# Plain f32 products for attention's projection and merge in a fused alignment, attention and expert kernel

## The reference

```
h = grad of the soft Needleman-Wunsch value of theta (32 x 128 x 128)
h = h + attention(layernorm(h))
h = h + experts(layernorm(h))        # 8 experts, top 2, silu gated
```

```
Q = einsum('bthd,hd->bht', xh, Wq);  K = einsum('bthd,hd->bht', xh, Wk)
P = softmax(-(Q[:, :, :, None] - K[:, :, None, :]) ** 2 / 4)
O = einsum('bhts,bhse->bhte', P, einsum('bthd,hde->bhte', xh, Wv))
out = O.reshape(B, T, E) @ Wm + x
```

## Time and profile before

| | us |
|---|---|
| median of 3 runs | 842.27 (841.99 to 842.51) |
| the profiled execution, its own time | 846.1 |
| its span | 844.0 |
| TensorE products busy | 484.8 (57%) |
| TensorE weight loads busy | 422.3 (50%) |
| VectorE busy | 593.4 (70%) |
| ScalarE busy | 406.8 (48%) |
| GpSimd busy | 230.7 (27%) |

### The profile page before, as it was taken

The page is one execution under the profiler, slowest core; times in us unless marked ns, Lnnn a source line. Parts: engine busy times, 40 slices in busy tenths (PEclk is TensorE's granted clock), DMA queues, the critical chain, the costliest instruction groups (busy, mean ns, idle before and its releaser), DMA issues.

```text
span 844.0 us, 13480 instructions
## 1 busy us (share of the span) xinstructions
PE 484.8 (57%) x2622; PEld 422.3 (50%) x2623; DVE 593.4 (70%) x2029; ACT 406.8 (48%) x1180; POOL 230.7 (27%) x417
## 2 busy tenths in 40 slices
PE   1200000000004689899899998620899999999960
PEld 0200000000003578798788987610688888888850
DVE  3698989889747866978988674652466666666645
ACT  1344444444302867666666574100566656666630
POOL 1054545455300000000403312455133333333330
PEclk9999999999999999999999999999999999999985
DMA  4499230403254122222102000012111111111109
GB/s 98 90 177 165 45 72 10 82 1 81 41 137 125 51 75 63 63 75 62 52 26 67 26 7 20 26 38 64 35 45 42 44 43 44 41 43 43 44 16 287
DMA packets 113385, 54.18 MB, mean 64 GB/s; under 512 B 56652, under 2 KB 109132, under 8 KB 113251
## 3 DMA queue, kind: packets, MB, share of 16 engines
q1 hardware_dynamic: 106366, 44.60, 22.7%
q0 software_dynamic: 4352, 8.47, 3.0%
q10 hardware_dynamic: 2621, 0.62, 0.5%
HBM read 29.93 MB, written 24.26 MB: 64 GB/s over the span
## 4 chain that ended last, share of the span: by engine, by line
PE 36%; DVE 31%; issue 20%; DMA 5%; SPq 4%; ACT 3%; ACTq 0%; DVEq 0%; POOLq 0%
DVE D L1178 5%; PE ps L541 5%; DVE D L1153 5%; PE ps L543 5%; PE ps L542 5%; PE ps L747 4%; PE ps L627 4%; PE ps L727 4%; PE ps L632 3%; ACT D L819 2%; DVE D L1144 2%; PE ps L746 2%; PE ps L743 2%; DVE rc L1322 2%; DVE ps L1133 1%
## 5 line engine op out<-in xcount | busy, mean ns | idle before, releaser
L1038 POOL DMA_INDIRECT xd_dram<-pay,slot x64 | 64.8, 1013 | 281.3 <-DVE pay L1402 263.9
L632 PEld LDWEIGHTS ps<-va,pt 128*128 128x128 f32 x512 | 137.5, 351 | 0.0
L627 PE MATMUL ps<-eye_sb,sq 128*128 128x128 f32 x256 | 114.8, 454 | 13.9 <-DVE on L1339 10.3
L1064 POOL DMA_INDIRECT y_dram<-on,dest x72 | 70.7, 982 | 164.1 <-DVE on L1482 127.5
L632 PE MATMUL ps<-va,pt 128*128 128x17 f32 x512 | 114.7, 307 | 0.0
L577 PE MATMUL ps<-zdiag,ones_f 32*128 32x32 f32 x2 | 0.6, 406 | 193.0 <-DVE zdiag L1221 193.0
L627 PEld LDWEIGHTS ps<-eye_sb,sq 128*128 128x128 f32 x256 | 87.5, 343 | 34.4 <-issue 25.8
L577 PEld LDWEIGHTS ps<-zdiag,ones_f 32*128 32x128 f32 x2 | 0.5, 304 | 193.1 <-DVE zdiag L1221 193.1
L1022 POOL TENSOR_TENSOR D<-D 128x128 f32<-128x128 f32 x130 | 56.3, 433 | 129.3 <-DVE D L1171 65.0
L1453 DVE TENSOR_TENSOR sq<-sq,ps 128x512 f32<-128x512 f32 x72 | 49.5, 688 | 56.2 <-PE ps L543 41.1
L819 ACT ACTIVATE D<-D 64x2 f32<-64x2 f32 (+1 forms) x154 | 31.4, 204 | 106.9 <-DVE D L1153 86.9
(11 more groups left out here) (226 smaller groups left out, 1474.1 us busy)
## 6 DMA issues: line engine op xcount, KB each, us to landing
stage<-xd_dram SPq DMA_DIRECT2D x72, 65.0 KB, 1.8
D<-th_dram SPq DMA_DIRECT2D x16, 208.0 KB, 4.8
g_dram<-D SPq DMA_DIRECT2D x14, 208.0 KB, 4.6
x_dram<-D SPq DMA_DIRECT2D x14, 208.0 KB, 4.7
h0q<-g_dram SPq DMA_DIRECT2D x8, 256.0 KB, 3.0
gb<-g_dram SPq DMA_DIRECT2D x8, 256.0 KB, 3.5
xf<-x_dram SPq DMA_DIRECT2D x8, 256.0 KB, 3.2
xb<-x_dram SPq DMA_DIRECT2D x8, 256.0 KB, 3.5
```

Of the source, the lines that this page charges most:

```text
L627: last = nc.tensor.transpose(ps[:, 5 + h // 4, T * (h % 4):T * (h % 4) + T], sq[n % 3][:, T * h:T * h + T], eye_sb[:])
L632: m = nc.tensor.matmul(ps[:, 7, (HD + 1) * h:(HD + 1) * (h + 1)], pt[turned % 2][:, T * h:T * h + T], va[q % 2][:, k, h, :], start=True, s ...
L1038: pool.indirect_dma_start(xd_dram, bass.IndirectOffsetOnAxis(slot[:, q, j, k:k + 1], 0), pay[q % 2][:, k, j, :], None).then_inc(s_sc[2 * k ...
L1064: pool.indirect_dma_start(y_dram, bass.IndirectOffsetOnAxis(dest[:, c:c + 1], 0), yrow[c], None, bounds_check=2 * NB * T - 1, oob_is_err=F ...
```

## The change

The operands of `project` and `merge` are no longer split. ScalarE's copies write plain f32 (`xnt`, `ont`), the subtractions `tokens_low` and `heads_low` and their semaphores go, and each block of a quad takes one f32 product: in `merge` with the whole 128 x 128 `wm_sb`, in `project` with a `wqk_sb` of 32 columns whose result goes to partitions 32k to 32k+31 of PSUM, one tile of 32 columns of the array per block. The weights are loaded as they are, `wqk_pl` as 128 x 32 in place of 4 x 128 x 128. TensorE waits once for `wm_sb` before its loop. The expert stage gets buffers of its own instead of the shared ones.

```diff
-        wqk_hi = sb("wqk_hi", [E, 4, 128], fr)
-        wqk_lo = sb("wqk_lo", [E, 4, 128], fr)
-        wm_hi = sb("wm_hi", [E, E], fr)
-        wm_lo = sb("wm_lo", [E, E], fr)
+        wqk_sb = sb("wqk_sb", [E, 32])
+        wm_sb = sb("wm_sb", [E, E])
...
-        xcol_hi = [ont_hi[:, T * k:T * k + T] for k in range(2)]
-        xcol_lo = [ont_lo[:, T * k:T * k + T] for k in range(2)]
+        xcol_hi = [sb(f"xcol_hi{k}", [128, T], fr)[:, :] for k in range(2)]
+        xcol_lo = [sb(f"xcol_lo{k}", [128, T], fr)[:, :] for k in range(2)]
...
-        hidt_hi, hidt_lo = xnt_hi, xnt_lo
+        hidt_hi = [sb(f"hidt_hi{k}", [128, 512], fr) for k in range(2)]
+        hidt_lo = [sb(f"hidt_lo{k}", [128, 512], fr) for k in range(2)]
...
                 pe.wait_ge(s_xnt, q + 1)
-                pe.wait_ge(s_xntl, q + 1)
                 need(pe, s_msk, q - 4)
                 for k in range(4):
-                    c = slice(T * k, T * k + T)
-                    m = three(ps[:, 2, 0:T], (wqk_hi[:, k, :], wqk_lo[:, k, :]), (xnt_hi[r][:, c], xnt_lo[r][:, c]),
-                              k == 0, k == 3)
+                    m = nc.tensor.matmul(ps[32 * k:32 * k + 32, 2, 0:T], wqk_sb[:], xnt[r][:, T * k:T * k + T],
+                                         start=True, stop=True)
...
                     c = slice(T * k, T * k + T)
-                    m = three(ps[:, 1, c], (ont_hi[:, c], ont_lo[:, c]), (wm_hi[:], wm_lo[:]))
+                    m = nc.tensor.matmul(ps[:, 1, c], ont[:, c], wm_sb[:], start=True, stop=True)
...
             pe.wait_ge(s_consts, 5)
+            pe.wait_ge(s_wraw, 1)
...
-            nc.scalar.activation(wqk_hi[:], raw_qk[:], ACT.Copy)
             nc.scalar.activation(below_sb[:], raw_below[:], ACT.Copy)
             act.wait_ge(s_small, 3)
-            nc.scalar.activation(wm_hi[:], ps[:, 1, 0:E], ACT.Copy).then_inc(s_wraw, 1)
+            nc.scalar.activation(wm_sb[:], ps[:, 1, 0:E], ACT.Copy).then_inc(s_wraw, 1)
...
-            dve.wait_ge(s_wraw, 1)
-            V_.tensor_tensor(wqk_lo[:], raw_qk[:], wqk_hi[:].bitcast(f32), ALU.subtract)
-            V_.tensor_tensor(wm_lo[:], ps[:, 1, 0:E], wm_hi[:].bitcast(f32), ALU.subtract)
...
-                quad(heads_low, n, -6)
-                quad(tokens_low, n, 7)
```

More of the change, by code:

```diff
@@ L123, in tower @@
         mz = al("mz", [128, 1])
-        raw_qk = al("raw_qk", [E, 4, 128])
         raw_v = al("raw_v", [E, E])
@@ L162, in tower @@
         xn = [sb(f"xn{k}", [T, 4, T]) for k in range(2)]
-        xnt_hi = [sb(f"xnt_hi{k}", [128, 512], fr) for k in range(2)]
-        xnt_lo = [sb(f"xnt_lo{k}", [128, 512], fr) for k in range(2)]
+        xnt = [sb(f"xnt{k}", [128, 512]) for k in range(2)]
         on = [sb(f"on{k}", [T, 4, T]) for k in range(2)]
-        ont_hi = sb("ont_hi", [128, 512], fr)
-        ont_lo = sb("ont_lo", [128, 512], fr)
+        ont = sb("ont", [128, 512])
         x3t = sb("x3t", [128, 512])
@@ L256, in tower @@
         s_thw = [sem(f"s_thw{c}") for c in range(BLKS)]
-        s_xntl = sem("s_xntl")
-        s_ontl = sem("s_ontl")
         s_qkh = sem("s_qkh")
@@ L641, in turn_heads @@
                 pe.wait_ge(s_xnt, min(q + 4, NQ))
-                pe.wait_ge(s_xntl, min(q + 4, NQ))
                 need(pe, s_x3t, q - 1)
@@ L650, in merge @@
                 pe.wait_ge(s_ont, q + 1)
-                pe.wait_ge(s_ontl, q + 1)
                 need(pe, s_h1, q)
@@ L661, in turn_inputs @@
                 pe.wait_ge(s_ont, min(q + 2, NQ))
-                pe.wait_ge(s_ontl, min(q + 2, NQ))
                 need(pe, s_rkc, q)
@@ L680, in ranks @@
                 pe.wait_ge(s_ont, min(q + 3, NQ))
-                pe.wait_ge(s_ontl, min(q + 3, NQ))
                 nc.tensor.matmul(ps[:, 0, 0:32], below_sb[:], msk[:, :, :].rearrange("p b e -> p (b e)"),
@@ L788, in _ @@
                 act.dma_start(dst, src).then_inc(s_in, 16)
-            for dst, src in ((raw_qk[:], wqk_pl.rearrange("g e c -> e g c")), (raw_v[:], wv_bd), (raw_m[:], w_m),
+            for dst, src in ((wqk_sb[:], wqk_pl), (raw_v[:], wv_bd), (raw_m[:], w_m),
                              (wg_sb[:], w_g), (eye_sb[:], eye), (raw_below[:], below), (mask_sb[:], head_mask),
@@ L873, in tokens_high @@
                 need(act, s_qkp, q - 1)
-                nc.scalar.activation(xnt_hi[q % 2][:], ps[:, 0, :], ACT.Copy).then_inc(s_xnt, 1)
+                nc.scalar.activation(xnt[q % 2][:], ps[:, 0, :], ACT.Copy).then_inc(s_xnt, 1)
             def values(q):
@@ L910, in heads_high @@
                 need(act, s_rp, q)
-                nc.scalar.activation(ont_hi[:], ps[:, 0, :], ACT.Copy).then_inc(s_ont, 1)
+                nc.scalar.activation(ont[:], ps[:, 0, :], ACT.Copy).then_inc(s_ont, 1)
             def copy_inputs(q):
@@ L1300, in first_norms @@
                 V_.tensor_tensor(h1[:, 4 * q:4 * q + 4, :], h[:], x1[q % 2][:], ALU.add).then_inc(s_hx, 1)
[L1302 to L1306, removed]
             def queries_keys(q):
@@ L1340, in normalise @@
                                  over(rc[:, 1, :], HD), ALU.mult).then_inc(s_on, 1)
[L1342 to L1345, removed]
             def residual(q):
@@ L1533 @@
     NH, HD = wq.shape
-    wqk_pl = np.zeros((4, 128, 128), wq.dtype)
+    wqk_pl = np.zeros((128, 32), wq.dtype)
     wv_bd = np.zeros((128, 128), wv.dtype)
@@ L1538 @@
         r = slice(HD * h, HD * h + HD)
-        for g in range(4):
-            for part in range(2):
-                wqk_pl[g, r, 32 * g + NH * part + h] = wq[h]
-                wqk_pl[g, r, 32 * g + NH * (2 + part) + h] = wk[h]
+        for part in range(2):
+            wqk_pl[r, NH * part + h] = wq[h]
+            wqk_pl[r, NH * (2 + part) + h] = wk[h]
         wv_bd[r, r] = wv[h].T
```

## The result

The new kernel takes 823.88 us (median of 4 runs, 822.7 to 824.96) against 842.38 (4 runs, 841.99 to 842.51) on the same chip: ratio 0.9781, 95% interval 0.9764 to 0.9798, 18.5 us faster. I had put 832.6, in a range from 828 to 838.5. The direction was right; the gain was nearly twice the 9.7 that I had worked out.

What follows compares the result with a forecast made beforehand. Attention was taken as bound in turns by TensorE (around project) and VectorE (from an odd turn's end through the norms). Gains 4.8+6.0-1.1 = 9.7 us off the median 842.27 gave 832.6 us, range 828 to 838.5.

Steps and rivals of the forecast that it cites:

- VectorE's low parts: Attention: dropping VectorE's two subtractions per quad shortens waits before turns 1, 2, 6, 10, 14, 18; gain 4.8 us.
- 1.1+0.6+1.0: Gains in us from dropping the tokens' subtraction in quads 0, 1 and 2, at the start of attention.
- the four gaps: TensorE's idle gaps before turns 6, 10, 14, 18, expected to close by 0.42, 0.60, 0.52, 0.60 us.
- I take four back to back: Project on TensorE: four narrow products at 0.36 us each, slot 1.74 instead of 2.73; 6.0 us saved over six intervals.
- 0.72 less 0.27: Project: price of a narrow product began from a 0.72 us f32 product, less 0.27 for one moving column versus 128.
- the rival on the column tiles: Project: the four column tiles overlap, slot 0.93 us, total gain 12.6, time 829.7; chance 0.22.
- so 0.72: Merge: one plain f32 product costs 0.72 us, read from the setup; merge 0.3 longer, 1.1 us lost in all.
- The lower bound that I had given, 0.45: Merge: lowest price in us considered for one plain f32 product, from a setup product with one moving column.
- The cap of 1.17: Intervals after turns 14, 18, 22, where VectorE also does `choose`: project's gain limited to 1.17 us each.
- What I said of hiding: Merge's extra 0.3 us hidden after turn 7, 0.17 showing after turns 11, 15, 19; setup savings and last merge hidden.
- The end is paced by the sends: End of attention: last norms wait 5.54 us for GpSimd's sends; what counts is how much earlier turn 31 is done.
- The clock rival: Attention: TensorE's clock rises as plain f32 products stream longer, some 20 us gained, time 822; chance 0.05.

Runs made afterwards that it cites:

- e14: New kernel with the merge as two fp32r terms, the heads' low part left out, five executions beside the unchanged new kernel: 824.6 us, ratio 0.9805.
- e6: New kernel with project as four plain f32 products of all 128 columns, weights zero-padded, no column tiles: 830.3 us, ratio 0.9868.
- e4: New kernel plus five series of eight products in TensorE's idle time of the alignment, to price product kinds: 829.8 us in one execution, ratio 0.980.
- e2: Kernel before with only the merge made plain f32 and the heads' subtraction dropped; project keeps three terms and its subtraction: 842.8 us, ratio 0.9949.
- e10: New kernel plus 40 plain f32 products in TensorE's idle time ahead of the experts, on a slower chip: 830.2 us, ratio 0.9808.
- e11: New kernel with VectorE's subtraction of the heads and its waits put back, result unread, the tokens' one left out: 833.7 us, ratio 0.9839.
- e5: New kernel with the merge as two fp32r terms, the heads' low part left out, first run: 826.3 us, ratio 0.9824.

## Why the prediction was wrong

The ledger of the starts of turns, trace of before against e14 (its merge is eight fp32r passes, and its attention stays at the low clock): a step's gain is how much shorter its intervals became.

| step | predicted | measured |
|---|---|---|
| VectorE's low parts (turns 1, 2, 6, 10, 14, 18, 22) | 4.8 | 4.8 |
| `project` (intervals after 2, 6, 10; 14, 18; 22) | 6.0 | 3 x 2.05 + 1.1 + 1.2 + 2.0 = 10.5 |
| `merge` (after 23; 27; 11, 15, 19) | -1.1 | 0.86 + 0.85 + 0 = 1.7 |
| sum | 9.7 | 17.0 |

With the plain f32 merge the two intervals gain 0.75 and 0.74 at the low clock (e6), 1.5 in place of 1.7. The medians of e14 and the kernel before on that chip are 17.1 apart. e14's lead at turn 31 is 19.7; the other 2.7 us lie in the intervals that end with turns 26, 27 and 30 (0.6, 0.3, 1.8), most of it where the trace of before has its two waits. On the first chip the gain was 18.5; the 1.5 left are within what the clock may be worth and the scatter of the runs.

- **VectorE's low parts: right**, each to about 0.1 us. The lead at turn 2 is 2.59, where I had 1.1+0.6+1.0 = 2.7; the four gaps closed by 0.39, 0.59, 0.49, 0.60, and turn 22's by 0.12.
- **The failed step is "I take four back to back", 1.74 for the slot of `project`.** It is 0.58. I had built a narrow product from 0.72 less 0.27, two numbers of lone products between changes of shape, and set them in a row. In fact the four overlap, as the rival on the column tiles had it. Even that rival, slot 0.93, was 0.35 too long: it was added up from the same two lone prices. (The Trainium skill, "TensorEngine Tiling (Array Packing)", Overview and Key Properties, which gives up to four times for 32-column tiles, agrees with e4: 0.43 against 0.11 a product. It also names a drain at each change of mode. From `project`'s last pass to the distances it is 0.35 with tiles and was 0.35 without, but the distances, with 32 rows, are a change of mode from either; no run here tells a drain from a change of shape.)
- **The price of the merge was the second failed step**, "so 0.72", from the earlier trace rows. A plain f32 product costs 0.43 in a row, so four are shorter than twelve fp32r ones, 1.84 against 2.73, of which the interval after turn 27 keeps 0.74 in e2, at the lower clock. The lower bound that I had given, 0.45, was the right end. (The Trainium skill, "FP8 and Floating Point Precision", TensorE Precision Notes, has four passes for true FP32; e4's series shows two per product at the length of an fp32r pass, and the measurement decides.)
- **The cap of 1.17** held after turns 14 and 18, with 1.13 and 1.16. After turn 22 it did not, with 2.03: VectorE was in time there. On the two slower chips it held there too, with 1.13 in e4 and 1.04 in e10; why is open. With `heads_low` put back (e11) the gain after turns 14 and 18 falls to 0.54 and 0.56.
- **What I said of hiding held.** The merge's gain behind turns 11, 15 and 19 is idle time of TensorE (1.37 us ahead of turn 20). The setup gave nothing. The end is paced by the sends: VectorE's last norms wait 6.27 us for them at 536.71, where before they waited 5.54. That wait did not eat the gain, as the last sends start as much earlier as turn 31 does.
- **The clock rival** came true as a mechanism and not as a price. The records go to the higher level right after plain f32 merges. But what it gives is in part idle time: in the new kernel's profile, in the higher stretch after turn 24, VectorE works without a pause (457.0 to 461.7), ScalarE waits 1.58 us for its `mn`, and TensorE sits idle for 2.30 us ahead of the logits at 461.80. What is left of the lead was not in the medians.
- The page's trace of before is 3.8 us over its median, and I took the sum off the median. The named steps add up to the gain of the medians, 17.0 and 17.1. The spans of the two traces are 22.4 apart: beside the 17.0 there are the 2.7 above, 2.3 between turn 31 and the first expert column, and 0.8 behind it, less 0.4 ahead of attention. The trace of before looks like those of the slower chips: it has the remote waits, and from its last send to the first expert column it takes 7.8 us, where the eight traces of the faster chips have 5.2 to 5.4 and the other traces of slower ones 5.9 to 9.5. No trace of before has a time near 842, so that the gain of the medians is these steps and nothing else is argued, not shown.

## What to carry to other kernels

Read a price from a row in which the instruction stands among its own kind, or take off the changes of shape at both ends: a lone product's start-to-start time held 0.29 us that a series doesn't pay. Products with 32 stationary columns belong into four column tiles (0.11 us a product here, against 0.43 in one tile). A subtraction that is hidden behind TensorE is hidden only as long as TensorE is slow; cost it again after every other term of the sum.

## What the runs showed that I had not expected

- At TensorE's lower clock a plain f32 product of 128x128 by 128 columns took 0.43 us against 0.21 for fp32r and 0.64 for three terms. Plain f32 is cheaper than the three-term split, and needs no subtraction.
- The granted clock went to its higher level after merges of plain f32, in all eight when they were doubled, and after none in e5 and e14, with as many fp32r passes in their place. It was not after every one: in the three traces of the new kernel, after six, three and six of the eight. In the higher stretch the distances took 0.73 us instead of 1.22, and a transpose 0.30 instead of 0.45.
- Without a clock record a stretch's column reads 1.00, although TensorE works at the lower level; the durations tell. Where there are records, the durations agree with them (a transpose takes 0.30 us at 1.00 and 0.45 at 0.50). So the 1.00 in the earlier trace rows was a missing record, and not an unreliable one.
